# A graph network kernel: GpSimd's gather of the source rows of x waits for the tally and the first rank

## The chip, the cores and the metric

The kernel runs on one core of a Trainium2 chip. The metric is the device time of one execution in microseconds (us); lower is better. The engines are TensorE (PE in the profile; PEld is its loading of weights), VectorE (DVE), ScalarE (ACT), GpSimd (POOL) and SyncE (SP).

## The reference, cut to what matters

There are 100,000 nodes with 64 float32 features, and 50,000 edges, sorted by `dst`, with random `src`.

```python
h = maximum(layernorm(x), 0)
msg = h[src] * edge_weight[:, None]
agg = segment_sum(msg, dst, 100000)
x = x + agg @ W_neigh + b_neigh + h @ W_self.T
h = maximum(layernorm(x), 0)           # only its number of rows is used
# second layer, over the rows that src names:
s, m, c = segment_sum(attr, src), segment_max(attr, src), counts(src)
z = concat([s, where(c > 0, m, 0), s / maximum(c, 1), u[0]])
x = x + relu(z @ W1 + b1) @ W2 + b2
```

## The kernel before, in words

Edges lie in SBUF as 128 partitions by NT = 400 columns ("tiles" of 128 edges); GT = 8 tiles make a group, and there are NG = 50 groups. The program is a row of blocks; all engines meet at the end of a block before the next one starts. Each block is called a stage here.

**Stage 1.** SyncE loads `src`, `dst`, the weights of the edges and the small matrices. GpSimd makes constants (memsets, iotas), signals `made["const"]`, waits for `made["srcs"]` (VectorE's copy of `src` as indices, L613) and gathers: `gather` (L592 to L597) runs 49 times; each waits until the buffer `xb[b]` has been stored (`x_kept[b]`), copies 8 columns of indices (L595) and issues 8 indirect DMAs (L597), each of which fetches 128 rows of x, one for each partition, into `xb[b]`. There are two buffers. SyncE stores each buffer to `x_of_src` in HBM (`keep`, L533), after it has waited for `gathered[b]`. In the same loop of SyncE stand the loads of the edge attributes into `rows` (L540, one for two groups; L544 and L545 after the loop).

Beside that VectorE splits the codes of each edge (source lane, source node, destination) into two digits of 5 bits and makes one-hot tiles from them, six for each group (L272, L273); TensorE multiplies them (L681, 24 matmuls for each group, accumulated over all groups), which gives the histograms of three keys: the tally. VectorE makes start positions from them (L641 to L655). Then `rank_dve`, `rank_pe` and `rank_act` give each edge its position in the order by source lane: the first rank, 50 groups, each a chain of TensorE (L332 to L357), ScalarE (L374 to L380) and VectorE (L290 to L318). The last operation of a group writes 8 columns of `idx_lane` (L318) and adds one to the semaphore `r_lane["idx"]`. VectorE ends the stage with small products and the copy L673, which waits for all attribute loads. Nothing in the tally or the rank reads what the gather brings, and the gather reads nothing of theirs.

**Stage 2.** GpSimd scatters the attribute rows to HBM by lane (`scatter_rows`, 391 indirect DMAs, L413), fed by ScalarE's copies (`stage_rows`, L406 and L407). Beside it the messages are computed: SyncE loads `x_of_src` again, VectorE and ScalarE normalise, TensorE transposes and multiplies by `W_neigh` (L468, L833), SyncE stores `message`.

**Stage 3.** The rows come back by lane, a second rank orders them by node, and GpSimd scatters them again (391 indirect DMAs), group by group as the indices come.

**Stage 4.** Running sums and maxima along the sorted rows, and the small network, give `mlp_row`.

**Stage 5.** 98 windows of 1024 nodes: load x, normalise, add the message rows and the network's rows by one-hot matmuls (L1334), store.

Of the kernel before, what the change touches and what calls it, by code (L numbers as in the profile page):

```python
# [67 lines left out]
def graph_layers(nc, x, src, dst, attr, weight, w_neigh, b_neigh, w_self, u, w1, b1, w2, b2, out):  # L68
# [8 lines left out]
    NG = 2 * (-(-(FT + 1) // (2 * GT)))  # L77
# [11 lines left out]
    with ctx:  # L89
# [145 lines left out]
        def own_waits(eng, name):  # L235
            owns[name].eng = eng
            return owns[name]
# [17 lines left out]
        def ranking(name):  # L255
            return {s: sem(f"{name}_{s}") for s in (
                "oh", "done", "eq", "same", "h", "h_used", "t", "t_used", "ohT", "w", "begin", "look", "idx")}
# [233 lines left out]
        r_lane, r_dst, r_node = ranking("lane"), ranking("dst"), ranking("node")  # L491
# [12 lines left out]
        with nc.Block() as block:  # L504
# [49 lines left out]
            @block.gpsimd  # L554
            def _(pool):
                own = own_waits(pool, "pool")
                nc.gpsimd.memset(src_i[:, :], -1)
                nc.gpsimd.memset(dst_i[:, :], -1)
                nc.gpsimd.memset(code_i[:, :], -1)
                nc.gpsimd.memset(next_i[:, :], N)  # L560
                nc.gpsimd.memset(ew[:, :], 0.0)
                nc.gpsimd.memset(wn2[:, :], 0.0)
                nc.gpsimd.memset(wsT2[:, :], 0.0)
                nc.gpsimd.memset(fill[:, :, :], 0.0)
                own(nc.gpsimd.memset(rows[:, FT:NT, :], 0.0))
                own(nc.gpsimd.memset(fill[:, :, KEY:RM], -1.0))
                pool.sem_inc(made["pads"], 1)
                for t, full in ((ident, False), (identb, False), (identh, False), (later, True)):
                    own(nc.gpsimd.memset(t[:, :], 2048.0 if full else 0.0))
                    if full:  # L570

                        own(nc.gpsimd.affine_select(out=t[:, :], in_=t[:, :], compare_op=ALU.is_ge, fill=0.0,
                                                    base=0, pattern=[[-1, P]], channel_multiplier=1))
                    else:
                        own(nc.gpsimd.affine_select(out=t[:, :], in_=t[:, :], compare_op=ALU.not_equal, fill=1.0,
                                                    base=0, pattern=[[-1, P]], channel_multiplier=1))
                own(nc.gpsimd.memset(before[:, :], 1.0))
                own(nc.gpsimd.affine_select(out=before[:, :], in_=before[:, :], compare_op=ALU.is_gt, fill=0.0,
                                            base=0, pattern=[[1, DIGIT]], channel_multiplier=-1))
                for t, pattern in ((iota_d, [[1, DIGIT]]), (iota_n, [[1, P]]), (first_of, [[P, NW + GT]])):  # L580
                    own(nc.gpsimd.iota(t[:, :], pattern, base=0, channel_multiplier=0,
                                       allow_small_or_imprecise_dtypes=True))
                own(nc.gpsimd.memset(chain_mask[:, :, :], 1.0))
                own(nc.gpsimd.memset(chain_mask[:, :, 0:1], 0.0))
                own(nc.gpsimd.memset(eps_t[:, :], EPS))
                own(nc.gpsimd.memset(ones[:, :], 1.0))
                own(nc.gpsimd.memset(ones_b[:, :], 1.0))
                for b in range(2):
                    own(nc.gpsimd.memset(a_st[b][:, :, :], 1.0))
                pool.sem_inc(made["const"], 3)  # L590

                def gather(g, b, count):  # L592
                    pool.wait_ge(x_kept[b], count * 16)
                    pool.sem_inc(paced["pool"], 1)
                    own(nc.gpsimd.tensor_copy(gx_idx[b][:, :], idx_src[:, bass.ds(g * GT, GT)]))  # L595
                    for k in range(GT):
                        nc.gpsimd.indirect_dma_start(  # L597
                            out=xb[b][:, k, :], out_offset=None, in_=x,
                            in_offset=bass.IndirectOffsetOnAxis(ap=gx_idx[b][:, k:k + 1], axis=0)).then_inc(gathered[b], 16)

                pool.wait_ge(made["srcs"], 1)
                with pool.Fori(0, FG // 2) as i:
                    own.loop(i, 2)
                    for b in range(2):
                        gather(i * 2 + b, b, i + 1)
                    own.end(FG // 2)
                gather(FG, 0, FG // 2 + 1)
# [887 lines left out]
```

## Time and profile before

| what | us |
|---|---|
| timed executions, median of 2 | 3069.18 |
| their lowest and highest | 3063.62 and 3074.75 |
| profiled execution, span from first to last instruction | 3664.4 |

The span is the only time that the profiled execution has; it is 595 us above the median of the timed ones. "Issue" in the profile is time in which an engine waited for nothing that the profile shows, and "remote" is a signal whose giver it does not name. Stage 1 lasts in the profiled execution to about 1007 us, stage 2 to 1605, stage 3 to 2262, stage 4 to 2935.

### The profile page before, as it was taken

Reading aid. Unit: us, or ns where it says so; the run is one execution under the profiler, and the core shown is the slowest. Engines: PE = TensorE matmul, PEld = TensorE weight load, DVE = VectorE, ACT = ScalarE, POOL = GpSimd, SP = SyncE. Lnnn points to the kernel's source line nnn. Section 1 sums busy time; section 2 is a strip of 40 time slices with the busy share of each in tenths; the row PEclk is TensorE's granted clock in tenths of the full one; section 3 lists DMA queues with packets and bytes.
Section 4 is the critical chain, followed back from the end, with each engine's and each line's share of the span. In section 5 each row is a group of like instructions: output and inputs, shape, how many; then the busy total and the mean of one; then the engine's idle time right before and its main releaser. Section 6 shows DMA issues by size and latency. Waiting matters only on the chain. (4 is left out here: it accounts for less than half of the span.)

```text
span 3664.4 us, 61138 instructions
## 1 busy us (share of the span) xinstructions
PE 1730.4 (47%) x16412; PEld 1365.9 (37%) x16413; DVE 2081.8 (57%) x4430; ACT 706.4 (19%) x1434; POOL 1692.1 (46%) x2048
## 2 busy tenths in 40 slices
PE   0000003666522222223333332599999967676666
PEld 0000002444422221222222221476677756665555
DVE  2000007666654454434333332488888879999998
ACT  0000000222111111111111111244444422222221
POOL 6766761000077776735655555111111146556564
PEclk9999999855555555555555555689989875667777
DMA  2222220000022221220000001111111147777775
GB/s 58 61 57 57 62 57 12 0 0 0 0 70 70 67 72 55 69 98 10 10 10 10 10 10 62 35 30 33 30 30 32 31 110 169 161 160 165 163 166 118
DMA packets 503986, 221.85 MB, mean 61 GB/s; under 512 B 457140, under 2 KB 470778, under 8 KB 503706
## 3 DMA queue, kind: packets, MB, share of 16 engines
q1 hardware_dynamic: 316067, 140.61, 14.8%
q0 software_dynamic: 53376, 44.40, 5.6%
q10 hardware_dynamic: 134520, 36.58, 4.8%
q8 instruction: 8, 0.13, 0.0%
q14 instruction: 15, 0.12, 0.0%
HBM read 130.32 MB, written 90.66 MB: 60 GB/s over the span
## 5 line engine op out<-in xcount | busy, mean ns | idle before, releaser
L413 POOL DMA_INDIRECT by_node<-row_st,idx_st x391 | 384.0, 982 | 291.5 <-ACTq L408 174.4
L413 POOL DMA_INDIRECT by_lane<-row_st,idx_st x391 | 401.4, 1027 | 167.5 <-issue 124.8
L597 POOL DMA_INDIRECT xb<-in_x_dram,gx_idx x392 | 373.5, 953 | 162.6 <-issue 146.8
L1260 POOL DMA_DIRECT2D rows<-mlp_row x490 | 251.2, 513 | 281.2 <-PE ps L1334 177.0
L1334 PE MATMUL ps<-rows,work 96*128 96x64 bf16 x4704 | 245.9, 223 | 209.2 <-DVE work L1288 209.1
L681 PE MATMUL ps<-oh_lo,oh_hi 128*32 128x32 bf16 x1200 | 66.3, 189 | 574.7 <-issue 431.2
L272 DVE TENSOR_TENSOR oh_hi<-iota_d,hi_b_lane 128x256 bf16<-128x256 bf16 x101 | 41.4, 410 | 517.2 <-remote 300.5
L972 POOL COPY s_st<-sign_b 128x384 bf16 (+1 forms) x99 | 71.0, 717 | 566.0 <-ACTq L1134 514.1
L1334 PEld LDWEIGHTS ps<-rows,work 96*128 96x128 bf16 x4704 | 225.6, 118 | 251.8 <-DVE work L1288 248.2
L681 PEld LDWEIGHTS ps<-oh_lo,oh_hi 128*32 128x32 bf16 x1200 | 47.4, 103 | 593.3 <-issue 441.0
L1288 DVE TENSOR_TENSOR work<-iota_n,near 96x1024 bf16<-96x1024 f32 x196 | 257.4, 1313 | 3.4
L357 PE MATMUL ps<-begin_p,ohT 32*128 32x32 bf16 x1600 | 113.4, 235 | 282.3 <-DVE begin_p L302 144.2
L468 PE MATMUL ps<-ident,h 128*128 128x128 f32 x588 | 140.8, 385 | 212.5 <-DVE h L453 141.3
L473 ACT ACTIVATE hT<-ps 128x512 f32<-128x512 f32 x147 | 87.8, 597 | 728.6 <-PE ps L468 472.5
L305 DVE TENSOR_TENSOR prod<-ps,oh_lo 128x256 f32<-128x256 f32 x100 | 42.4, 424 | 324.3 <-PE ps L357 161.3
L398 POOL DMA_DIRECT2D spare<-eps_t x4 | 2.2, 556 | 461.7 <-POOLq L504 443.2
L357 PEld LDWEIGHTS ps<-begin_p,ohT 32*128 32x128 bf16 x1600 | 98.3, 118 | 288.7 <-issue 201.8
L833 PE MATMUL ps<-wn,hT 128*128 128x128 f32 x392 | 101.6, 441 | 220.5 <-ACT hT L473 133.7
L468 PEld LDWEIGHTS ps<-ident,h 128*128 128x128 f32 x588 | 93.8, 197 | 230.9 <-DVE h L453 154.0
L833 PEld LDWEIGHTS ps<-wn,hT 128*128 128x128 f32 x392 | 87.2, 327 | 240.2 <-ACT hT L473 146.5
L374 ACT ACTIVATE hist<-ps 32x256 f32<-32x256 f32 x100 | 37.2, 372 | 706.3 <-PE ps L342 407.1
L1323 PE MATMUL ps<-wsT,hT 128*128 128x128 f32 x784 | 171.0, 387 | 0.7 <-ACT hT L473 0.7
(196 smaller groups left out, 4667.8 us busy)
## 6 DMA issues: line engine op xcount, KB each, us to landing
rows<-message SPq DMA_DIRECT2D x784, 36.4 KB, 2.2
rows<-in_x_dram SPq DMA_DIRECT2D x97, 256.0 KB, 3.5
out_dram<-rows ACTq DMA_DIRECT2D x97, 256.0 KB
mlp_row<-v_row SPq DMA_DIRECT2D x97, 194.0 KB
message<-m_row SPq DMA_DIRECT2D x48, 388.0 KB
rows<-mlp_row POOLq DMA_DIRECT2D x490, 36.4 KB, 2.4
x_of_src<-xb SPq DMA_DIRECT2D x49, 256.0 KB
xb<-x_of_src SPq DMA_DIRECT2D x49, 256.0 KB
```

The lines of the kernel that those rows point to most:

```text
L357: last = nc.tensor.matmul(g_ps[:, k, :], ohT[b][:, k, :], begin_p[b][:, part, :, k], start=(part == 0), stop=(part == 1))
L413: nc.gpsimd.indirect_dma_start(out=table, out_offset=bass.IndirectOffsetOnAxis(ap=idx_st[b][0:parts, k:k + 1], axis=0), in_=row_st[b][0:pa ...
L468: last = nc.tensor.transpose(ps[3 * b][:, P * k:P * k + P], h[b][:, 2 * k:2 * k + 2, :].rearrange("p a c -> p (a c)"), ident[:, :])
L473: nc.scalar.activation(hT[b][:, :, :], ps[3 * b][:, :].rearrange("p (k c) -> p k c", c=P), ACT.Copy).then_inc(done, 1)
L597: nc.gpsimd.indirect_dma_start(out=xb[b][:, k, :], out_offset=None, in_=x, in_offset=bass.IndirectOffsetOnAxis(ap=gx_idx[b][:, k:k + 1], a ...
L681: last = nc.tensor.matmul(ps[c][0:DIGIT, 0:DIGIT], oh_hi[b][:, c, k, :], oh_lo[b][:, c, k, :], start=(first and k == 0), stop=(final and k ...
L833: last = nc.tensor.matmul(ps[1 + b][:, P * k:P * k + P], hT[b][:, k, :], wn2[:, :], start=True, stop=True)
L972: nc.gpsimd.tensor_copy(s_st[b][:, :, :], sign_b[:, bass.ds(g * QT, QT)].unsqueeze(2).to_broadcast([P, QT, KU]))
L1260: pool.dma_start(chunk[b][0:CH, 1, k0 + k, :], mlp_row[bass.ds(pool.snap(at[k]), CH), :]).then_inc(own_loaded[b], 16)
L1288: nc.vector.tensor_tensor(pick[c][0:CH, n, :, :], iota_n[0:CH, :].unsqueeze(1).to_broadcast([CH, GT, P]), near[c][0:CH, n, :].unsqueeze(2) ...
L1323: last = nc.tensor.matmul(ps[4 + b][:, P * k:P * k + P], hT[b % 2][:, k, :], wsT2[:, :], start=False, stop=(k == 3))
L1334: last = nc.tensor.matmul(ps[4 + b][:, D * k:D * k + D], pick[b % 2][0:CH, n, k, :], parts[b][0:CH, n, k, D * part:D * part + D], start=(n ...
```

## The change

GpSimd waits, before its first gather, until `r_lane["idx"]` has reached NG = 50, which it does when the last group of the first rank is done. Nothing else is changed.

```diff
                 pool.wait_ge(made["srcs"], 1)
+                pool.wait_ge(r_lane["idx"], NG)
                 with pool.Fori(0, FG // 2) as i:
                     own.loop(i, 2)
                     for b in range(2):
                         gather(i * 2 + b, b, i + 1)
```

## Rows read from the trace of the kernel before

**Rows 1.** The page, busy tenths in 40 equal slices (91.6 us each).

```profile
DVE  2000007666654454434333332488888879999998
POOL 6766761000077776735655555111111146556564
```

**Rows 2.** Busy time in stretches of the span, by stage.

```profile
core 0: us, PE busy (x) PEld busy (x) DVE busy (x) ACT busy (x) POOL busy (x), PEclk, DMA share, GB/s
18.00:564.00 546.00, 36.63 (x344) 21.76 (x345) 34.35 (x97) 0.00 (x0) 383.31 (x441) 1.00 0.26 58
564.00:1007.00 443.00, 255.81 (x3364) 193.50 (x3363) 323.61 (x992) 73.38 (x152) 0.07 (x1) 0.71 0.00 1
1007.00:1605.00 598.00, 156.30 (x588) 122.28 (x588) 282.94 (x588) 98.31 (x247) 403.67 (x395) 0.50 0.24 76
1605.00:2262.00 657.00, 235.90 (x2500) 166.16 (x2500) 253.71 (x755) 97.77 (x248) 375.97 (x383) 0.52 0.05 10
2262.00:2935.00 673.00, 558.62 (x3578) 428.69 (x3578) 501.97 (x945) 281.13 (x472) 111.81 (x203) 0.85 0.13 38
2935.00:3664.00 729.00, 487.10 (x6038) 433.52 (x6038) 678.73 (x1035) 155.78 (x315) 408.45 (x592) 0.70 0.71 152
```

**Rows 3.** Timeline, 19 to 29 us: start, duration, engine, line, operation.

```profile
19.19 1.31 POOL L597 DMA_INDIRECT xb<-in_x_dram,gx_idx  x1 [1.00 <-POOL gx_idx L595]
...
21.29 0.42 DVE L272 TENSOR_TENSOR oh_hi<-iota_d,hi_b_lane 128x256 bf16<-128x256 bf16 x1 [0.34 <-DVE dst_f L631]
...
23.31 0.42 DVE L272 TENSOR_TENSOR oh_hi<-iota_d,hi_b_lane 128x256 bf16<-128x256 bf16 x1
...
28.77 0.94 POOL L597 DMA_INDIRECT xb<-in_x_dram,gx_idx  x1 [0.30 <-issue]
```

**Rows 4.** Waits, 18 to 564 us: total, times, longest.

```profile
PE ps L681 <- issue: 424.4, 159, 23.4
DVE oh_hi L272 <- remote: 292.5, 7, 65.1
DVE oh_hi L272 <- issue: 211.6, 4, 64.4
POOL xb L597 <- issue: 146.8, 384, 2.2
POOL xb L597 <- remote: 12.9, 4, 3.7
```

**Rows 5.** Timeline of TensorE, from 50 us.

```profile
50.73 0.19 PE L681 MATMUL ps<-oh_lo,oh_hi 128*32 128x32 bf16 x1 [0.51 <-issue]
52.13 0.19 PE L681 MATMUL ps<-oh_lo,oh_hi 128*32 128x32 bf16 x1 [1.20 <-issue]
```

**Rows 6.** Line L597: duration in ns min/median/max, first and last start.

```profile
L597 POOL DMA_INDIRECT xb<-in_x_dram,gx_idx x392: 938/944/1313, 19.2 to 563.1; - x196
```

**Rows 7.** Last one-hot of the tally (timeline), and line L318.

```profile
639.80 0.41 DVE L273 TENSOR_TENSOR oh_lo<-iota_d,lo_b_node 128x256 bf16<-128x256 bf16 x1
...
L318 DVE SCALAR_TENSOR_TENSOR idx_lane<-pos_part x50: 166/166/168, 655.9 to 1002.0; 128x8 int32 x50
```

**Rows 8.** Timeline: the last DMA of the gather and its last store.

```profile
563.12 0.94 POOL L597 DMA_INDIRECT xb<-in_x_dram,gx_idx  x1 [0.30 <-issue]
...
566.64 0.34 SPq L533 DMA_DIRECT2D x_of_src<-xb  x1
```

**Rows 9.** Groups by line: the two scatters and the gather.

```profile
L413 POOL DMA_INDIRECT by_node<-row_st,idx_st x391 | 384.0, 982 | 291.5 <-ACTq L408 174.4
L413 POOL DMA_INDIRECT by_lane<-row_st,idx_st x391 | 401.4, 1027 | 167.5 <-issue 124.8
L597 POOL DMA_INDIRECT xb<-in_x_dram,gx_idx x392 | 373.5, 953 | 162.6 <-issue 146.8
```

**Rows 10.** Waits in stage 3, 1605 to 2262 us.

```profile
ACT hist L374 <- remote: 299.3, 20, 16.7
POOL by_node L413 <- ACTq L408: 174.4, 30, 26.4
```

## The prediction

> **What bounds the kernel now.** I read the slices of the page first. GpSimd (POOL) is busy at 6 to 7 tenths from the start to about 560 us, then not at all for four slices, and in exactly those slices VectorE (DVE) wakes up [rows 1]. The table by stage says it in numbers: from 18 to 564 us GpSimd is busy 383 us and VectorE 34 of 546; from 564 to 1007 GpSimd does nothing and VectorE is busy 324 [rows 2]. So in the profiled execution the gather and the tally with its rank stand almost one behind the other, although nothing in the code orders them. Of VectorE's 97 instructions before 564, 7 are set-up and 90 are one-hots, six to a step: 15 of the 50 tally steps. The other 35 and the whole rank come after it.
>
> What holds the tally back is no semaphore. It starts at full pace beside the gather: two steps are 21.29 to 23.31, 2.0 us each [rows 3]. Some 9 us after the first indirect DMA, TensorE (PE) begins to stall. The list of waits gives it 424 us of "issue", that is, waiting for nothing that the profile shows, and VectorE 292 + 212 us behind it [rows 4]; single matmuls of one accumulation group, between which the program has no wait, come 0.7 or 1.4 us apart [rows 5]. GpSimd itself keeps an even pace: 392 indirect DMAs with a median of 944 ns, from 19.2 to 563.1 us [rows 6].
>
> **Which time counts.** The profiled execution has 3664.4 us of span and no other time of its own; the two timed executions have a median of 3069.18, 595 us less. Work that GpSimd paces, or that VectorE fills, cannot shrink that much: the last stage has VectorE busy 679 of 729 us, the one before it 502 of 673 with TensorE at 559 [rows 2]. What can shrink is stalls. If the tally and rank run free beside the gather, stage 1 ends with the gather, near 569 us, where the profile has 1007: 438 us less. Stage 3 (657 us) has ScalarE waiting 299 us for late signals and GpSimd 174 us for ScalarE [rows 10]; of the 174, 26.4 are the start, and without the other 148 it would be near 509, but some refills remain, so I take 546: 111 less. Stage 2 (598) has 391 scatters of 1027 ns with 0.30 between [rows 9], 519 us, and some 26 around them: 53 less. 438 + 53 + 111 = 602 against the 595 missing. I therefore take it that the stalls of TensorE belong to the profiled execution, and that in the timed runs GpSimd's 546 us hide the tally and the rank completely.
>
> **The change, part by part.** One wait is added on GpSimd. It costs nothing itself; all that GpSimd issues is behind it: 49 copies of indices and 392 indirect DMAs. Behind these, on SP's queue, stand 49 stores of x_of_src and all attribute loads but the first, since each store waits for its gather. The last attribute load is waited for by one copy on VectorE (L673, 0.53 us), so stage 1 ends a few us after the gather, as now.
>
> When does GpSimd start? The tally's first one-hot is at 21.3; 50 steps of 2.01 us are 100.6, so it ends at 121.9. From the last one-hot (639.8 + 0.4) to the first index of the rank (655.9) are 15.7 us, and from the first to the last index 346.1 us [rows 7]. The set-up on VectorE up to 21.3 stays as it is [rows 3]. Sum: 21.3 + 100.6 + 15.7 + 346.1 = 483.7, 484 with the last signal. Most steps and the whole rank ran with GpSimd silent, which is the state they will have. The gather started at 18.0; it moves by 484 - 18 = **466 us**. Its own length cancels out as long as it ended stage 1 before, and so does the tail behind it (last DMA at 563.1, last store issued at 566.6, [rows 8]).
>
> What comes back? The gather no longer shares its time with VectorE. Beside the free tally its first eight DMAs took 19.19 to 29.71, 10.52 us, where 8 of 0.944 and 7 gaps of 0.30 make 9.65: 0.11 us more for each [rows 3]. Over all 392 that is 43 us, the upper end; nothing is the lower end. The scatters beside the other rank average 982 ns against the gather's 953, 0.03 more [rows 6, 9]. With 76 DMAs beside the tally at 0.11 and 316 at 0.03 I take 8 + 9 = 17 us, rounded to 18. Net: 466 - 18 = 448, and between 423 and 466 by these bounds.
>
> The tally, the rank, and the set-up of constants lose the gather as neighbour, but they are now on the path whole. The later stages start later and are otherwise untouched: stage 2 is paced by GpSimd's scatters and reads x_of_src and the indices, both complete. **3069 + 448 = 3517 us.**
>
> The Trainium skill, "SBUF — State Buffer", section "Who interferes with whom", speaks for the relief and against a clean sum: GpSimd and VectorE share a port pair as an exclusive lock, and one of them blocks wholly. By that rule the relief would come from VectorE's copies and two-input operations, and the 0.11 us above would be its size; the trace bears out no more than that.
>
> **The rivals.** *B, the stalls are real.* Then the timed runs serialise gather and rank as the profile does, and the change only swaps their order. In the profile's numbers stage 1 ends at 484 + 546 + 5 = 1035 less the excess that GpSimd shows (12.9 us of waits for signals and some 30 of issue above 0.30 each, [rows 4]), 992 to 1035 against 1007, that is -15 to +28. Time: about 3075, from 3054 to 3097, so not slower by a measurable amount. For it: the stall is seen, 424 us of it, and it begins and ends with the indirect DMAs. Against: then the 595 us have no home; they would have to be 0.5 us on each of the 1174 indirect DMAs, though these show a fixed 944 ns with hardly any spread. The Trainium skill, "NOTIFIC — the notification-queue block", section "10. Constraints, capacities, measured rates", speaks for B: it says that writing an implicit record costs the engine nothing. By that rule recording can't be what stalls TensorE, and the time would be near 3075; no run here shows it yet, and the 595 us speak against it.
>
> *C, half of each.* The timed gather is shorter (say 1.10 us per DMA and not 1.39) and the rank beside it suffers some 100 us, so that the rank ended stage 1, at about 584. After: 484 + 431 + 5 = 920, 336 more: 3405.
>
> *D, faster.* The hold frees both sides: the stalls are real, and the gather alone also drops its waits and 43 us of sharing. 484 + (546 - 43 - 43) + 5 = 949 against 1007: 3069 - 58 = 3011, just about the limit of 2%. It needs every small term on one side.
>
> That the hold does nothing is excluded: the semaphore reaches 50 only with the last group of the rank.
>
> **How the numbers follow.** A, the forecast: 0.78. C and its like, 0.05. B 0.12, D 0.05. A and C are slower by over 2% (61 us, about what a measurement can tell here): 0.83 with rounding to 0.82; B is within 2%, and takes a little more, 0.14; D leaves 0.04 for faster. A's own range is 3069 + 423 = 3492 to 3069 + 466 = 3535, widened by 20 for the spread of the two timed runs (11 us) and for a slightly different pace of the rank in a timed run: 3472 to 3555. Downward I go on towards C, to 3400. B and D lie outside, 0.17.
>
> **What would show it.** In the profile of the changed kernel GpSimd is silent from about 18 to 484 us, the tally steps come every 2.0 us from 21 us on, the idx_lane rows run from about 138 to 484, and no "issue" wait of TensorE above a few us stands before 484. The gather then runs 484 to about 1020, alone, with VectorE at nothing. That profile's span should hardly differ from 3664 (within 30 us), although the timed runs are 448 us slower: the two kernels differ in the timed runs by what the profile had already lost. If the timed runs are slower by under 60 us, the step that took the stalls for a matter of the profiled execution is wrong. If the profile has the gather faster than 520 us, the relief was set too low.

## The result, and the profile after

The changed kernel takes 3499.24 us (two executions, 3498.61 and 3499.87) against 3069.18: 430 us more, a ratio of 1.142 with a 95% interval of 1.137 to 1.147. The forecast was 3517, from 3400 to 3555.

One thing has to be said at once, since no number below can be read without it. **The same kernel runs in one of two conditions: in one TensorE stalls beside GpSimd's indirect DMAs, in the other it does not.** In the first the kernel before has medians of 3660 to 3698 us (single executions 3650 to 3714), in the second of 3062 and 3069 (3055 to 3075). No series of runs mixed the two, and none of the numbered chips was seen in both: chips 1, 6 and 10 stalled (chip 10 in two series), chip 8 did not. I call them the stalling and the free chips, though it is not shown whether the chip or its state at the time decides. The result and the profile after come from a free chip, whose number is not on record. The profile shown ahead of the prediction has the stalls and, with a span of 3664.4 us, the length of the stalling kind; I take it that it was made on a stalling chip, which no record says.

The page of the changed kernel, busy tenths in 40 slices of 87 us; to compare with [rows 1]:

```profile
DVE  8776730000015555535444442788888879999998
POOL 0000037777767777765777771111111155656564
PEclk9755555555555555555555655898999967777777
```

The two halves of stage 1 have changed places. VectorE starts at once with 8 tenths, and GpSimd starts in the sixth slice. The stretches of that profile, by stage, with the columns of [rows 2]:

```profile
0.00:485.00 485.00, 266.55 (x3704) 202.51 (x3705) 361.24 (x1102) 73.14 (x152) 8.89 (x36) 0.68 0.01 3
485.00:1021.00 536.00, 1.27 (x4) 1.00 (x4) 1.64 (x6) 1.00 (x1) 381.01 (x441) 0.50 0.26 59
1021.00:1580.00 559.00, 156.37 (x588) 122.28 (x588) 280.18 (x589) 100.96 (x247) 405.55 (x395) 0.50 0.26 81
1580.00:2100.00 520.00, 224.93 (x2500) 166.50 (x2500) 255.25 (x761) 97.75 (x248) 380.88 (x387) 0.54 0.06 13
2100.00:2773.00 673.00, 562.33 (x3595) 432.29 (x3596) 502.29 (x941) 282.92 (x476) 109.25 (x200) 0.85 0.13 38
2773.00:3496.00 723.00, 460.84 (x6023) 407.73 (x6022) 665.60 (x1033) 154.96 (x312) 403.12 (x592) 0.75 0.72 153
```

From 485 to 1021 VectorE is busy for 1.64 us: nothing is left that could hide behind the gather. Stages 2 and 3 are short here, 559 and 520 us against 598 and 657 in [rows 2], with the same work; that is the free chip and not the change. The cuts between stages are good to some 10 us. GpSimd's second scatter, which fills stage 3, can be compared without a cut. Its rows, first in the kernel before, then in the changed one, then in a kernel on chip 8, a free chip, whose gather starts at once and has half the DMAs (described below):

```profile
L413 POOL DMA_INDIRECT by_node<-row_st,idx_st x391: 904/969/1269, 1623.3 to 2271.6; - x196
L413 POOL DMA_INDIRECT by_node<-row_st,idx_st x391: 900/969/1268, 1597.2 to 2104.3; - x196
L413 POOL DMA_INDIRECT by_node<-row_st,idx_st x391: 900/969/1271, 1067.0 to 1574.2; - x196
```

From the first to the last of these DMAs it is 648, 507 and 507 us; from ScalarE's first operation of stage 2 (at 1008.0, 1021.3 and 491.2) to the first of them 615, 576 and 576. The two kernels on free chips, one with the change and one without, agree to the microsecond, so the change slows nothing in stages 2 and 3. What is left from the last of these DMAs on, stages 4 and 5, is 1392.8 us in the profile before and 1392.5 in the one after.

The last index of the rank, the gather behind it, and the end of the stage, from the same profile (the lines of idx_lane and of the gather, then the timeline):

```profile
L318 DVE SCALAR_TENSOR_TENSOR idx_lane<-pos_part x50: 166/167/168, 137.3 to 483.5; 128x8 int32 x50
L597 POOL DMA_INDIRECT xb<-in_x_dram,gx_idx x392: 938/944/1187, 485.4 to 1014.0; - x196
```

```profile
484.19 0.19 POOL L595 COPY gx_idx<-idx_src 128x8 uint32 x1 [473.00 <-DVEq L320]
...
1009.84 0.52 DVE L674 COPY rows<-src_f 128x400 f32<-128x400 f32 x1 [522.67 <-DMA rows<-in_edge_attr_dram]
...
1017.49 0.34 SPq L533 DMA_DIRECT2D x_of_src<-xb  x1
1020.00 1.28 ACT L859 ACT_TABLE_LOAD   x1 [540.76 <-PEq L504]
```

GpSimd stood 473 us at the new wait, released by L320, the signal after the last index (L318). Then the gather takes 484.2 to 1014.9, 531 us. VectorE's copy (L674, L673 before) waits 523 us for the last attribute load, which SP could not issue earlier because its stores wait for the gather; it costs nothing beside the gather, which ends later still. The stage ends at 1020.

### The profile page after: what moved, and what is told of

The parts are those of the page before. It is cut to its first block and busy times, and to the rows that moved or that the text cites. A ratio compares the mean times of both kernels' runs of the same rounds, so it can differ in the third digit from the quotient of the medians.

```text
span 3496.8 us, 61139 instructions
## 1 busy us (share of the span) xinstructions
PE 1672.3 (48%) x16412; PEld 1332.3 (38%) x16413; DVE 2066.2 (59%) x4430; ACT 710.7 (20%) x1434; POOL 1688.7 (48%) x2048
## 5 line engine op out<-in xcount | busy, mean ns | idle before, releaser
L413 POOL DMA_INDIRECT by_lane<-row_st,idx_st x391 | 403.8, 1033 | 127.4 <-issue 115.8
L597 POOL DMA_INDIRECT xb<-in_x_dram,gx_idx x392 | 370.9, 946 | 149.9 <-issue 110.3
L1335 PE MATMUL ps<-rows,work 96*128 96x64 bf16 x4704 | 234.6, 218 | 216.9 <-DVE work L1289 216.9
L1335 PEld LDWEIGHTS ps<-rows,work 96*128 96x128 bf16 x4704 | 214.3, 115 | 257.2 <-DVE work L1289 254.2
L674 DVE COPY rows<-src_f 128x400 f32<-128x400 f32 x1 | 0.5, 523 | 522.7 <-DMA rows<-in_edge_attr_dram 522.7
L595 POOL COPY gx_idx<-idx_src 128x8 uint32 (+1 forms) x49 | 9.8, 201 | 473.1 <-DVEq L320 473.0
L445 DVE TENSOR_REDUCE stat<-sq 128x8 f32<-128x512 f32 x147 | 100.2, 682 | 220.6 <-ACT sq L458 220.6
L1075 PE MATMUL ps<-ident,a_st 128*96 128x128 f32 x792 | 131.5, 318 | 77.4 <-POOLq L979 75.3
L1324 PE MATMUL ps<-wsT,hT 128*128 128x128 f32 x784 | 156.3, 362 | 0.7 <-ACT hT L473 0.7
L1270 POOL TENSOR_TENSOR rows<-rows,biasb 128x512 f32<-128x512 f32 x98 | 150.3, 1534 | 7.0 <-DMA out_dram<-rows 6.0
L1075 PEld LDWEIGHTS ps<-ident,a_st 128*96 128x96 f32 x792 | 107.9, 191 | 102.3 <-POOLq L979 75.4
L332 PE MATMUL ps<-later,identh 128*128 128x512 f16 x200 | 124.0, 620 | 43.1 <-DVEq L283 43.1
L453 DVE SCALAR_TENSOR_TENSOR h<-xc,stat 128x512 f32<-128x512 f32 x147 | 139.5, 949 | 6.2 <-DVE stat L452 0.3
```

The costliest lines, as they stand in the source:

```text
L332: nc.tensor.matmul(bank[:, :].rearrange("p (k c) -> p k c", c=P), identh[:, :], later[:, :].unsqueeze(1).to_broadcast([P, 4, P]), start=Tr ...
L413: nc.gpsimd.indirect_dma_start(out=table, out_offset=bass.IndirectOffsetOnAxis(ap=idx_st[b][0:parts, k:k + 1], axis=0), in_=row_st[b][0:pa ...
L453: return nc.vector.scalar_tensor_tensor(h[b][:, :, :], xc[b][:, :, :], 0.0, wide(stat[b][:, 2, :]), ALU.max, ALU.mult)
L597: nc.gpsimd.indirect_dma_start(out=xb[b][:, k, :], out_offset=None, in_=x, in_offset=bass.IndirectOffsetOnAxis(ap=gx_idx[b][:, k:k + 1], a ...
L1075: nc.tensor.matmul(ps[0][0:KU, P * k:P * k + P], a_st[b][:, k, :], ident[:, :], start=True, stop=True)
L1270: nc.gpsimd.tensor_tensor(y[b][:, :, :], x_in[b][:, :, :], biasb[:, :].unsqueeze(1).to_broadcast([P, GT, D]), ALU.add).then_inc(w["biased" ...
```

## The experiments

**The kernel before again**, unchanged.

> The kernel before, unchanged, profiled again. Theory A (the 424 us of stalls on TensorE belonged to the one profiled execution, not to the program): the span is near 3068 us, tally steps come every 2.0 us from 21 us on beside the gather, the last index of the rank is near 484 to 500 us, the gather ends stage 1 near 585 to 590 us (the changed kernel's 1020 less the 430 by which it is slower), so the 392 indirect DMAs beside VectorE take about 36 us longer than the 531 us that they take alone. Rival B (the gather stalls TensorE in every execution): the profile again shows VectorE nearly silent beside the gather and stage 1 ends near 1007.

Measured: 3696.05 us (10 executions, 3688 to 3707), beside a kernel before of 3698.24 (25 executions). Theory A fell as it was worded: all these executions have the long time, and the profiled one has the stalls. Its list of waits from 1000 to 2350 us, which is stages 2 and 3 with their edges, has long waits for signals as [rows 10] has:

```profile
ACT hist L374 <- remote: 350.6, 30, 21.7
ACT hT L473 <- remote: 241.7, 18, 19.7
```

So the stall is no matter of one odd execution. It belongs to the chip on which the kernel runs, or to its condition at that time; the runs do not part the two.

**The mirror: the gather first, the tally behind it.**

```diff
                 own(nc.vector.tensor_copy(dst_f[:, :], dst_i[:, 0:NT]))
+                dve.wait_ge(gathered[0], (FG // 2 + 1) * (16 * GT))
                 with dve.Fori(0, TRIPS) as i:
```

> The mirror of the change: VectorE waits before the tally until all 49 groups of the gather have landed; GpSimd starts at 18 us as before. Theory A (the loss is the overlap, whichever goes first): gather alone 18 to about 549, landed near 552, then 462 us of tally and rank: stage 1 ends near 1017, and the time is 3495 to 3505, as slow as the change. Rival E (the loss comes from what the hold does to GpSimd's and SP's queues, or to the attribute loads): clearly nearer to 3069 than to 3499.

Measured, on the stalling chip: 3746.22 us against 3698.24, ratio 1.0137 (1.0094 to 1.0181). The forecast of 3495 to 3505 was for a free chip; it missed here, and theory A and rival E are not tested by it. Against E speak the rows of the changed kernel on the free chip: stage 1 ends 5 us behind the gather, and stages 2 and 3 are as long as without the change. Two rows of its timeline show the order:

```profile
561.65 0.94 POOL L597 DMA_INDIRECT xb<-in_x_dram,gx_idx  x1 [0.31 <-issue]
...
565.49 0.43 DVE L272 TENSOR_TENSOR oh_hi<-iota_d,hi_b_lane 128x256 bf16<-128x256 bf16 x1 [544.60 <-DMA xb<-in_x_dram,gx_idx]
```

With VectorE held 545 us, stage 1 ends at 1033, where the kernel before on the same chip has 1010. On a stalling chip the overlap is worth only these 23 us (the 15 tally steps of [rows 2] at 2.01 us are 30). The other 25 us of the 48 lie behind stage 1: 6 in the second scatter and 19 in stage 4. From GpSimd's last scatter to VectorE's first one-hot of stage 5 the profile of the kernel before on this chip (the run before_again) needs 713.5 us and this one 732.9. TensorE nearly fills that time, and its granted clock is a little lower here. Two stretches of 100 us each, first of the kernel before, then of the mirror:

```profile
2796.00:2896.00 100.00, 91.27 (x595) 69.95 (x594) 82.97 (x157) 46.29 (x78) 16.21 (x30) 0.90 0.12 31
2825.00:2925.00 100.00, 92.02 (x563) 70.12 (x563) 79.59 (x151) 43.81 (x74) 15.76 (x30) 0.85 0.11 29
```

TensorE is busy for 91 and 92 us in both, but does 595 matmuls at a clock of 0.90 and 563 at 0.85. Why a wait in stage 1 goes with a lower clock 1300 us later is open. Over all profiles of this case, stages 4 and 5 together take between 1383 and 1412 us.

**Holding for 1 and for 25 groups of the rank, not for 50.**

```diff
                 pool.wait_ge(made["srcs"], 1)
+                pool.wait_ge(r_lane["idx"], 1)          # and NG // 2
```

> GpSimd waits only for the first group of the first rank (index count 1 and not 50). Theory A: it starts at 138 us and not 18, so the gather moves by 120 us; the gather then runs beside the rank alone and is spared the tally, which gives back up to 10 us: 3179 to 3189. Rival F (the cost comes only once the gather is longer than what runs beside it, that is, there is slack): under 3100.

> GpSimd waits for 25 of the 50 groups of the rank. Theory A: it starts at 308 us, shift 290; of the 36 us of sharing about half is saved: 3335 to 3352. With hold_first and the change the cost would lie on a line of about 6.3 to 7.1 us for each group of rank waited for. Rival F: a cost that begins only at some number of groups.

Measured, on the same stalling chip: 3689.18 (ratio 0.9971, 0.9951 to 0.9990) and 3680.15 (0.9961, 0.9939 to 0.9983). Both forecasts, +110 to +283 us, missed by their whole size. They were made for a free chip; here there is almost no overlap to lose. The rank's index row of the second says how it goes, first in all and then for the stretch of the gather alone (309 to 860 us):

```profile
L318 DVE SCALAR_TENSOR_TENSOR idx_lane<-pos_part x50: 166/168/169, 137.3 to 982.8; 128x8 int32 x50
...
L318 DVE SCALAR_TENSOR_TENSOR idx_lane<-pos_part x7: 166/167/168, 314.1 to 794.4; 128x8 int32 x7
```

Seven groups of the rank in the gather's 546 us, where undisturbed ones take 7.06 us each. The hold for the most part only moves the same two blocks. Both kernels are even slightly faster than the kernel before, with intervals that end below 1: stage 1 ends 14 and 22 us earlier than there (ScalarE's first operation of stage 2 is at 997.4 and 988.9, and at 1011.3 in the kernel before). That fits what passes beside the gather: seven groups of the rank are worth 49 us, where the tally steps that pass in the kernel before are worth some 30. The line of cost per group held, which the theory expects of a free chip, was not measured.

**The change again, beside the kernel before.**

> The change, against the kernel before on one chip. The first runs left two conditions: in one the kernel before takes 3069 us, in the other, which the last four runs all had, 3698, and TensorE stalls beside every indirect DMA. Theory A2 (two conditions of the chip or the session, the change costs the lost overlap only where nothing stalls): where the kernel before takes 3698, the change is within 1.5% of it, 3690 to 3725; where it takes 3069, the change takes 3499. Rival G (the change itself removes the stalls, also in the later stages): near 3499 beside a kernel before of 3698, that is 5% faster.

Measured, on a second stalling chip: 3727.42 us against 3694.62, ratio 1.0102 (1.0067 to 1.0136). A2 holds in its condition of 1.5%, and its number is passed by 2 us: the same edit that costs 430 us on a free chip costs 33 here. G falls: the change does not remove the stalls. Its stretches:

```profile
485.00:1035.00 550.00, 1.27 (x4) 0.99 (x4) 1.65 (x6) 0.00 (x0) 381.35 (x440) 0.50 0.27 58
1035.00:1640.00 605.00, 156.33 (x588) 122.27 (x588) 281.58 (x588) 98.59 (x247) 403.58 (x395) 0.50 0.24 73
1640.00:2311.00 671.00, 241.50 (x2476) 166.81 (x2476) 248.27 (x740) 95.84 (x243) 378.24 (x380) 0.53 0.05 12
```

One kernel on two chips: the stage of scatters beside the messages takes 559 and 605 us, the one of scatters beside the second rank 520 and 671, the gather alone 536 and 550. GpSimd alone loses least, 14 us; the scatters that wait for the indices of the rank lose most, 151.

**Tally held for 8 groups of the gather.**

```diff
                 own(nc.vector.tensor_copy(dst_f[:, :], dst_i[:, 0:NT]))
+                dve.wait_ge(gathered[1], 4 * (16 * GT))
                 with dve.Fori(0, TRIPS) as i:
```

> VectorE waits before the tally for 8 groups of the gather, some 86 us. Where nothing stalls: tally and rank end at 484 + 86 = 570, still about where the gather ends (585 to 590), so no change: 3069 to 3075. Where TensorE stalls: the 8 groups pass with no tally step beside them, of which some 2 to 3 were done, 0 to +10 us on 3698. Rival H (in the fast condition the tally or rank ends the stage, and not the gather): 60 to 86 us slower than 3069.

Measured, on the stalling chip: 3724.89 against 3694.62, ratio 1.0089 (1.0052 to 1.0127), 30 us where 0 to 10 were expected. Stage 1 ends at 1016, 6 us later than in the profile of the kernel before on another stalling chip, within the forecast; the rest lies in later stages, most of it in stage 4 as with the mirror (728.0 us, where the next run on this chip has 716.2). Rival H, that tally or rank ends the stage on a free chip, is not tested by this run; the kernel with four DMAs below speaks to it.

**GpSimd's first gather 6 us earlier.**

```diff
                 sp.wait_ge(made["pads"], 1)
                 edge_load(sp, src_i, src, "src")
+                prime(sp, x_kept)
...
                 sp.wait_ge(made["const"], 1)
-                prime(sp, x_kept)
```

(with the memset of eps_t moved before `made["pads"]`)

> The small DMA that opens the two gather buffers goes out first in SP's queue, so GpSimd does not wait 6.7 us for it before its first gather. Theory A (the gather sets the end of stage 1 from its first DMA on): 5 to 7 us faster in either condition, which 3 rounds may not resolve beside 3698 but do beside 3069. Rival H: no change.

Measured, on the stalling chip: 3692.69 against 3694.62, ratio 0.9989 (0.9964 to 1.0013), not resolved. The row of the index copies, first and last start, shows that the gather did move by its 6.4 us, from 18.1 to 11.7 at its start and from 555.7 to 549.3 at its end:

```profile
L595 POOL COPY gx_idx<-idx_src x49: 191/202/240, 11.7 to 549.3; 128x8 uint32 x48, 128x8 uint32<-128x8 uint32 x1
```

**Half the rows in each indirect DMA.** The messages of half the edges are left out; zeros, set beforehand, stand in the other half of each buffer.

```diff
...
-                            out=xb[b][:, k, :], out_offset=None, in_=x,
-                            in_offset=bass.IndirectOffsetOnAxis(ap=gx_idx[b][:, k:k + 1], axis=0)).then_inc(gathered[b], 16)
+                            out=xb[b][0:P // 2, k, :], out_offset=None, in_=x,
+                            in_offset=bass.IndirectOffsetOnAxis(ap=gx_idx[b][0:P // 2, k:k + 1], axis=0)).then_inc(gathered[b], 16)
```

> Each of the 392 indirect DMAs fetches 64 rows and not 128; the other half of each buffer holds zeros, so the messages of half the edges are left out. Where TensorE stalls beside indirect DMAs: if the stall goes by the number of rows described, about twice as many tally steps (30 of 50) pass beside the gather for the same time, or the gather is shorter and stage 1 ends 60 to 200 us earlier; if it goes by the number of DMAs, TensorE stalls just as long for each DMA and 15 steps pass. Where nothing stalls: the gather takes 0.6 to 0.94 us for each DMA, and stage 1 ends with the rank at 484 to 500 where it is below 0.9.

Measured, on the stalling chip: 3688.26 against 3694.62, ratio 0.9985 (0.9961 to 1.0008). The gather's line and the list of waits beside it (18 to 560 us):

```profile
L599 POOL DMA_INDIRECT xb<-in_x_dram,gx_idx x392: 899/903/1148, 20.4 to 569.7; - x196
```

```profile
PE ps L683 <- issue: 381.4, 143, 24.2
DVE oh_hi L272 <- remote: 326.0, 12, 65.2
```

With 64 rows an indirect DMA takes 903 ns, with 128 944 [rows 6], and TensorE's 381 us of stall are nearly the 424 of [rows 4]. Beside this gather 19 of the 50 tally steps pass, where four profiles with 128 rows (before, before_again, before_third, prime_early) have 14 to 17; if the stall went by the rows, some 30 would have passed. So neither GpSimd's time nor the stall goes by the rows, or only to a small part. That the stall goes by the number of indirect DMAs fits this, but no run on a stalling chip changed that number.

**A plain DMA for each indirect one.** It reads consecutive rows of x; the rows that `src` names are left out.

```diff
-                        nc.gpsimd.indirect_dma_start(
-                            out=xb[b][:, k, :], out_offset=None, in_=x,
-                            in_offset=bass.IndirectOffsetOnAxis(ap=gx_idx[b][:, k:k + 1], axis=0)).then_inc(gathered[b], 16)
+                        nc.gpsimd.dma_start(xb[b][:, k, :], x[bass.ds((g * GT + k) * P, P), :]).then_inc(gathered[b], 16)
```

> Each of the 392 indirect DMAs is replaced by a plain DMA from GpSimd's queue of 128 consecutive rows of x, as many rows and bytes, no indices: the messages are made from other rows than src names. Where TensorE stalls (kernel before at 3698): if the stall needs the indirect form, tally and rank run free and stage 1 ends with them at 484 to 500 us, which is 3180 to 3210; if any DMA whose descriptors GpSimd writes does it, TensorE's tally still creeps and stage 1 ends with the length of the plain DMAs (some 0.5 to 0.9 us each, 250 to 400 us) plus 440, about 3400 to 3550. Where nothing stalls: 3069 less some 100, since the rank would end the stage.

> The plain DMAs in place of the indirect ones once more (messages are made from other rows), now for the slow condition of the chip, where the kernel before takes 3667 to 3698. If the stall of TensorE needs the indirect form, tally and rank end stage 1 at 484 to 490 us and the time is 520 us below the kernel before, some 3150 to 3180. If every DMA whose descriptors GpSimd writes stalls it, the plain DMAs last some 390 us (18 to 408 in the fast condition) with few tally steps beside them, then some 440: stage 1 ends near 850, 3500 to 3550. In the fast condition: 2972 again.

The first run met a free chip: 2971.82 us against 3062.16, ratio 0.970 (0.964 to 0.977). The second met a stalling one: 3160.48 against 3660.22, ratio 0.864 (0.857 to 0.870). There the plain form takes 500 us off, in the forecast's 3150 to 3180; the first run was forecast at some 100 us less and has 90. Its rows on the stalling chip, the index of the rank, the plain DMAs, and the stretches from the start of the gather:

```profile
L318 DVE SCALAR_TENSOR_TENSOR idx_lane<-pos_part x50: 166/167/169, 137.5 to 484.3; 128x8 int32 x50
...
L597 POOL DMA_DIRECT2D xb<-in_x_dram x392: 534/534/744, 19.0 to 406.5; - x196
```

```profile
18.00:490.00 472.00, 267.38 (x3708) 203.57 (x3708) 357.09 (x1088) 74.12 (x152) 319.88 (x442) 0.67 0.27 68
490.00:1110.00 620.00, 164.54 (x678) 128.25 (x679) 294.23 (x623) 101.49 (x255) 395.42 (x395) 0.51 0.23 73
1110.00:1760.00 650.00, 231.05 (x2413) 161.51 (x2410) 242.72 (x726) 94.36 (x240) 381.64 (x389) 0.53 0.05 10
```

Beside 392 plain DMAs of GpSimd's queue the last index of the rank starts at 484.3, within a microsecond of where it does with GpSimd silent (483.5). In the same execution the two stages with indirect scatters are long again, 620 and 650 us. Of the two forms tried only the indirect one brings the stall.

**Four of the eight indirect DMAs of each group.** Half the messages are left out; zeros, set beforehand, stand in their place.

```diff
...
-                    for k in range(GT):
+                    for k in range(GT // 2):
...
-                    sp.wait_ge(gathered[b], count * (16 * GT))
+                    sp.wait_ge(gathered[b], count * (8 * GT))
```

> Only 4 of the 8 indirect DMAs of each group are issued (196 and not 392), the rest of each buffer holds zeros, so half the messages are left out. Where TensorE stalls: gather of some 275 us with 7 to 8 tally steps beside it, then the rest alone: stage 1 ends near 735, the time is 3698 less 270, 3420 to 3440. Where nothing stalls: the gather ends near 300 and the tally and rank end the stage at 484 to 500: 3069 less 90 to 100, 2965 to 2985. Rival (the stall goes with the bytes or rows, as many rows of one DMA as of two): already half excluded by the DMAs of 64 rows, which stalled as long as those of 128.

Measured, on the free chip: 2970.01 against 3062.16, ratio 0.970 (0.963 to 0.977), in the forecast's 2965 to 2985. This is the overlap seen directly, in a kernel whose gather, tally and rank all start at the beginning:

```profile
L599 POOL DMA_INDIRECT xb<-in_x_dram,gx_idx x196: 940/964/1407, 20.0 to 311.2; - x196
...
L318 DVE SCALAR_TENSOR_TENSOR idx_lane<-pos_part x50: 166/167/170, 138.9 to 485.2; 128x8 int32 x50
```

```profile
50.52 0.82 PE L683 MATMUL ps<-oh_lo,oh_hi 128*32 128x32 bf16 x24 [1.20 <-DVE oh_lo L273]
52.53 0.82 PE L683 MATMUL ps<-oh_lo,oh_hi 128*32 128x32 bf16 x24 [1.19 <-DVE oh_lo L273]
```

Beside indirect DMAs TensorE's 24 matmuls of a tally step run in one piece, every 2.01 us, where [rows 5] has single ones 0.7 and 1.4 us apart. The rank keeps its pace too: until the gather is over at 312, 25 of its groups pass, the first index at 138.9 and the 25th at 308.7, which is 7.07 us for each, against the 7.06 with GpSimd silent. The rank ends at 485 and now ends the stage (490). And the plain DMAs give the same time, 2972: two ways of making the gather short stop at the same floor. Rival H does not fit this: tally and rank are not slowed beside indirect DMAs on a free chip, and with the whole gather they would end near 485 as well. In the kernel before it is thus the gather that sets the end.

**The kernel before a third time.**

> The kernel before once more, for a profile in the fast condition, if the chip is in it. There, by theory A: tally steps every 2.0 us beside the gather, last index of the rank at 484 to 490 us with no stall of TensorE, gather from 18 to 570 to 585 us with indirect DMAs of a mean of 0.98 to 1.02 us (0.946 alone in the changed kernel; 0.997 beside tally and rank with half the DMAs), stage 1 ends at 576 to 590 us, span 3060 to 3070. Rival: the rank is slowed and ends stage 1. In the slow condition: as the first profile, 3690 to 3700.

Measured: 3667.38 us (10 executions, 3650 to 3677), a third stalling chip, as forecast for that condition. No profile shows the kernel before on a free chip; the kernel with four DMAs stands in for it.

## Why the prediction was right

**Stage 1 of the kernel before is bound by the gather, and tally and rank are hidden.** Right, on the chips where the result was measured. Halving the gather took 92 us off, down to the rank's end. The sum says the same: the changed kernel ends stage 1 at 1020, and 430 less is 590, behind the rank's 484. Stages 2 and 3 hold none of the 430 us, since they are as long in the changed kernel as in the kernel with four DMAs.

**The rank ends at 484.** The last index starts at 483.5, GpSimd at 484.2. 100.6 + 15.7 + 346.1 from 21.3 was good to half a microsecond, since those rows had been taken with GpSimd silent.

**The relief, 18 us.** This term was mis-sized. 466 less 430 is 36, near the upper end (43). The kernel with four DMAs lets its two prices be checked. Its DMAs take 1.02 us beside the tally (20 to 122 us, 69.6 us busy over 68) and 0.97 beside the rank (125.8 over 129, to 312), against 0.946 (370.9 over 392) in the changed kernel, where nothing runs beside them: 0.08 and 0.03 us more, where the prediction had 0.11 and 0.03. Its 0.03 had been read from two different kinds of DMA, scatters against gather, and was right by luck. By these prices I estimate that a full gather, with some 72 DMAs beside the tally and 262 beside the rank, loses 6 + 8 = 14 us, less than the 18 taken. So the sharing that the rows show does not explain the 36, and the other 22 have no place. They need not lie in stage 1: the 430 is a difference of medians of two executions each, stages 4 and 5 differ by up to 29 us between profiles, and the kernel before on chip 8 is 7 us below the 3069.

**The budget of the 595 us.** Right in its size: 438, 53 and 111 us were taken off stages 1, 2 and 3, 602 in all. The rows above give 39 and 141 for stages 2 and 3 and nothing for 4 and 5, and 595 less these is 415 for stage 1, so the prediction had too much in the first two and too little in the third, and its sum came out partly by luck. But the step "the stalls of TensorE belong to the profiled execution" was wrong as it was put, and the forecast came out in spite of it, since the timed runs of the result happened to be on a free chip: on a stalling one the change costs 33 us, and 448 would have missed by some 400. The stalls go with the chip or its condition: every execution of the kernel before on three chips has the long time, and the profile after, which holds as many instruction records, has no stall. The sentence on the span (within 30 us of 3664) fell for that reason; it is 3496.8, and the timed value of the same execution is 3498.61.

**Rival B, the stalls are real.** It is true of the stalling chips. It gave -15 to +28 us for the change; there it is +33, 1.0%. The Trainium skill ("NOTIFIC — the notification-queue block", section "10. Constraints, capacities, measured rates") says that an implicit record costs the engine nothing. The profile after agrees, since 61,139 instructions were recorded on a free chip without a stall. It was a fair warning against my step, while its conclusion for the time did not follow.

**C and D** had no part in it: on a free chip neither the tally nor the rank is slowed beside indirect DMAs (C), and the change is faster nowhere (D).

## What to carry to other kernels

Before a profile is used to cost a change, compare its span with the timed median. When they differ by 20%, find which stages can hold the difference (one that an engine fills can't), and cost the change for both readings: here one edit was worth +14% or +1% by the chip. A wait that orders two independent pieces of work costs the start that it delays whenever the delayed piece sets the end of its stage; its own length cancels out. And two pieces that stand one behind the other in a profile are not proof that they can't overlap.

## What the runs showed of the hardware that was not expected

On three chips (1, 6 and 10) the other engines are held up beside GpSimd's indirect DMAs. Single matmuls with no wait between them come 0.7 us and multiples of it apart (50.03, 50.73, 52.13, 53.53 us in the profile before), and waits for a signal last up to 17 to 22 us in stages 2 and 3, and up to 65 us in the tally. SyncE is touched as well: the instruction that issues a store of x_of_src takes 0.34 us in the changed kernel on a free chip, and in the kernel before, on a stalling chip, from 0.004 to 1.40 with a median of 0.70. On a stalling chip, beside plain DMAs, it is 0.34 again. The three rows, in this order (changed, before, plain on chip 10):

```profile
L533 SPq DMA_DIRECT2D x_of_src<-xb x49: 332/338/383, 497.2 to 1017.5; - x49
L533 SPq DMA_DIRECT2D x_of_src<-xb x49: 4/700/1397, 31.5 to 566.6; - x49
L533 SPq DMA_DIRECT2D x_of_src<-xb x49: 332/338/383, 25.9 to 408.5; - x49
```

On chip 8, and where the result was measured, kernels with the same 782 indirect scatters show nothing of it. The stall came with the indirect form and not with the plain one (392 plain DMAs of GpSimd leave the rank at 484.3 us), and hardly less with half the rows (381 us of stall with 64, 396 to 427 with 128). What in the chip or its condition decides is open.

An indirect DMA of 64 rows takes GpSimd 903 ns, one of 128 rows 944 ns: nearly all of it does not depend on the rows. A plain one of 128 rows takes 534 ns.
